# A one-hot comparison that reads f32 numbers from PSUM, in a graph network kernel on one Trainium2 core

## The reference: what is computed

```python
h = relu(layernorm(x)); x = x + L0(h)   # two SAGE layers: mean of the messages h[src] per dst
h = relu(layernorm(x)); x = x + L1(h)   # two attention layers (8 heads)
h = relu(layernorm(x)); x = x + L2(h)   # a graph transformer layer
h = relu(layernorm(x)); x = x + L3(h)   # two GIN layers: max of the messages h[src] per dst
# SAGE: agg = segment_sum(h[src], dst) / max(deg, 1);  out = relu(agg @ Wl + b + h @ Wr)
# GIN:  agg = segment_max(h[src], dst);                out = (h + agg) @ W + b
```

## Time and profile before

| what | value |
|---|---|
| median of 3 runs | 8765.62 us (8765.36, 8765.62, 8808.96) |
| span of the profiled execution | 8795.7 us; of the three runs only 8808.96 can hold it |
| busy share PE, DVE, ACT, POOL | 35%, 64%, 26%, 74% |
| chain of waits: POOL line 1644 | 48% of the span |
| passes 0 and 1 | about 90 to 1120 and 1200 to 2250 us |
| attention passes 2 to 4 | about 2360 to 6510 us |
| passes 5 and 6 | about 6630 to 7645 and 7710 to 8725 us |

### The profile page before, as it was taken

The page is one execution under the profiler, slowest core; times in us unless marked ns, Lnnn a source line. Parts: engine busy times, 40 slices in busy tenths (PEclk is TensorE's granted clock), DMA queues, the critical chain, the costliest instruction groups (busy, mean ns, idle before and its releaser), DMA issues.

```text
span 8795.7 us, 77398 instructions
## 1 busy us (share of the span) xinstructions
PE 3081.9 (35%) x15108; PEld 1692.0 (19%) x15108; DVE 5587.2 (64%) x8739; ACT 2262.0 (26%) x6542; POOL 6501.0 (74%) x5372
## 2 busy tenths in 40 slices
PE   3666656666400000200000010000025676667766
PEld 1333333333200000000000000000023343333333
DVE  5556646666477777567777757777776555455554
ACT  1000000000244444344444434444441000000000
POOL 5787768888488888568887758888856777777776
PEclk9888868888655555555555555555557887777877
DMA  2222222222244444334444434444422222222222
GB/s 81 93 93 91 94 78 90 92 90 92 90 131 130 130 132 132 105 120 130 133 130 131 126 104 125 127 127 126 126 83 79 93 94 93 88 84 94 93 91 83
DMA packets 371813, 928.59 MB, mean 106 GB/s; under 512 B 107787, under 2 KB 140629, under 8 KB 371751
## 3 DMA queue, kind: packets, MB, share of 16 engines
q0 software_dynamic: 220208, 517.27, 20.8%
q1 hardware_dynamic: 151543, 410.66, 13.0%
HBM read 520.70 MB, written 406.64 MB: 105 GB/s over the span
## 4 chain that ended last, share of the span: by engine, by line
POOL 48%; issue 26%; PE 11%; another core or an unknown queue 7%; DVE 3%; DMA 2%; SPq 1%; ACT 1%; DVEq 0%; POOLq 0%; ACTq 0%
POOL arena L1644 48%; PE bank L1384 4%; PE cin_ps L1384 2%; PE cout_ps L1384 1%; DVE outs L652 1%; PE bank L1348 1%; PE bank L1335 1%; DMA arena<-table,near_idx 1%; PE bank L1373 1%; SPq L1537 0%; PE bank L1323 0%; PE bank L1349 0%; SPq L1586 0%; PE bank L1338 0%
## 5 line engine op out<-in xcount | busy, mean ns | idle before, releaser
L1644 POOL DMA_INDIRECT arena<-table,near_idx x5002 | 5982.2, 1196 | 1857.5 <-issue 1512.4
L1384 PE MATMUL bank<-arena,work 125*128 125x384 bf16 x6750 | 1428.7, 368 | 577.7 <-DVE work L667 294.7
L1361 PE MATMUL cin_ps<-ident,tails 128*128 128x128 f32 x9 | 2.7, 438 | 3988.8 <-DVE tails L905 3988.8
L652 DVE SCALAR_TENSOR_TENSOR outs<-outs,same,arena 128x128 f32<-128x128 f32 x1568 | 547.7, 349 | 682.3 <-DMA arena<-table,near_idx 518.6
L1136 ACT ACTIVATE arena<-bank,tile_base 125x128 bf16<-125x128 f32 x432 | 158.7, 367 | 3172.3 <-remote 1461.6
L1384 PEld LDWEIGHTS bank<-arena,work 125*128 125x128 bf16 x6750 | 709.4, 107 | 1218.9 <-issue 890.7
L741 DVE TENSOR_TENSOR work<-work,arena 128x896 f32<-128x896 f32 x336 | 370.1, 1102 | 716.1 <-DMA arena<-table,near_idx 713.5
L652 DVE SCALAR_TENSOR_TENSOR outs<-outs,fence,arena 128x128 f32<-128x128 f32 x1568 | 550.0, 351 | 420.8 <-DMA arena<-table,near_idx 212.0
L781 DVE TENSOR_TENSOR_SCAN work<-work 128x1024 f32<-128x1024 f32 x336 | 770.0, 2292 | 38.9
L1361 PEld LDWEIGHTS cin_ps<-ident,tails 128*128 128x128 f32 x9 | 1.5, 213 | 3989.9 <-DVE tails L905 3989.9
L667 DVE TENSOR_TENSOR work<-arena 125x3200 bf16<-125x3200 bf16 x378 | 689.0, 1823 | 51.1 <-issue 39.9
(11 more groups left out here) (237 smaller groups left out, 4890.7 us busy)
## 6 DMA issues: line engine op xcount, KB each, us to landing
rows_plain<-outs SPq DMA_DIRECT2D x448, 448.0 KB
rows_att<-outs SPq DMA_DIRECT2D x336, 504.0 KB
arena<-table,near_idx POOLq DMA_INDIRECT x5002
table<-arena SPq DMA_DIRECT2D x18, 500.0 KB
qtable<-arena SPq DMA_DIRECT2D x33, 250.0 KB
table<-H SPq DMA_DIRECT2D x24, 250.0 KB
arena<-qtable,near_idx POOLq DMA_INDIRECT x168
arena<-rows_plain,last_i POOLq DMA_INDIRECT x100, 3.3
```

Source lines behind the costliest of these rows:

```text
L652: v.scalar_tensor_tensor(out_plain[:, s, j, :], prev, flags[:, bass.ds(first + j, 1)], row, *ops).then_inc(s_agg, 1)
L1384: ins = pe.matmul(pick_bank[u], hot_src[k][u][:, t, :], parts3[:, :, t, :], start=(t == 0), stop=(t == NB - 1))
L1644: pool.indirect_dma_start(dst, None, tab, bass.IndirectOffsetOnAxis(ap=idx, axis=0))\
```

## The change

The one-hot comparison reads the turned source numbers in PSUM itself, as f32. Each partition's 25 own node numbers are laid once a pass in `node_no` (f32, 25 elements, read with a broadcast over the 128 edges), in place of the bf16 table `tile_no` of 25 x 128. ScalarE's Relu, the tile `pick_tile`, and the semaphore `s_tile` go. Since the comparison now holds the PSUM region, a turn may write a region only when the one-hot two groups back is done, which TensorE waits for; the regions alternate between two PSUM banks.

```diff
-        tile_no = arena[0:NP, TILE_AT:TILE_AT + NB * P // 2].bitcast(BF16).rearrange("p (i e) -> p i e", e=P)
-        PICK_AT = TILE_AT + NB * P // 2
+        node_no = arena[0:NP, TILE_AT:TILE_AT + NB]
+        PICK_AT = TILE_AT + NB
...
-        source_bank = [bank[0][0:NP, u * P:(u + 1) * P] for u in range(RING)] + [hist_ps[0:NP, 0:P]]
+        source_bank = {k: [(bank[0], cout_ps if k < 2 else flag_ps)[u % 2][0:NP, 384:512] for u in range(RING)]
+                       + [hist_ps[0:NP, 0:P]] for k in PICKS}
...
             def one_hot(k, it, s):
                 for i, (u, _) in enumerate(units(k, s)):
-                    v.wait_ge(s_tile, pick_number(k, it, s) + (i + 1))
-
-                    v.tensor_tensor(hot_src[k][u], pick_tile[u].unsqueeze(1).to_broadcast([NP, NB, P]), tile_no,
+                    v.wait_ge(s_across, pick_number(k, it, s) + (i + 1))
+
+                    v.tensor_tensor(hot_src[k][u], source_bank[k][u].unsqueeze(1).to_broadcast([NP, NB, P]),
+                                    node_no.unsqueeze(2).to_broadcast([NP, NB, P]),
                                     ALU.is_equal).then_inc(s_onehot, 1)
...
-                step(v.tensor_copy(tile_no, lo_iota[0:NP, 1:NB + 1].unsqueeze(2).to_broadcast([NP, NB, P])))
+                step(v.tensor_scalar(node_no, lo_iota[0:NP, 1:NB + 1], tile_base[0:NP, 0:1], None, ALU.subtract))
...
             def number_tiles(k, it, s):
-                n = pick_number(k, it, s)
                 for u, j in units(k, s):
                     at = it * (RING * GROUP) + (s * GROUP + j)
                     act.copy(pick_src[u], src_i[:, bass.ds(at, 1)].to_broadcast([P, NP])).then_inc(s_col, 1)
-                for i, (u, _) in enumerate(units(k, s)):
-                    act.wait_ge(s_across, n + (i + 1))
-                    act.activation(pick_tile[u], source_bank[u], ACT.Relu, bias=tile_base[0:NP, 0:1])\
-                        .then_inc(s_tile, 1)
...
                 for i, (u, _) in enumerate(units(k, s)):
                     pe.wait_ge(s_col, pick_number(k, it, s) + (i + 1))
+                    if not (isinstance(it, int) and it == 1 and s < 2):
+                        seen = pick_number(k, it, s - 1) if s else pick_number(k, it - 1, RING - 1)
+                        pe.wait_ge(s_onehot, seen)
                     pe.nop(nofuse=True)
-                    pe.matmul(source_bank[u], pick_src[u], ident[:, :], start=True, stop=True)\
+                    pe.matmul(source_bank[k][u], pick_src[u], ident[:, :], start=True, stop=True)\
                         .then_inc(s_across, 1)
```

## The result

The changed kernel took 8985.8 us in the median (8984.6 to 9002.8) against 8765.5 of the kernel before (8760.9 to 8809.0), a ratio of 1.024 with an interval of 1.022 to 1.026: 2.4% slower, where 5% faster had been forecast. The profiled execution's span is 9001.2 us.

What follows compares the result with a forecast made beforehand. POOL's indirect row fetches, held back by two-SBUF-input VectorE instructions, were taken as the bound. Gains of 150 (pass 1), 130 (pass 0), 157 (passes 5 and 6), 15 and 4 sum to 456 us: 8765.6 to 8310, range 8180 to 8600.

Steps and rivals of the forecast that it cites:

- What bounds the kernel, and the fetches: POOL's row fetches bound passes 0, 1, 5, 6; VectorE instructions with two SBUF inputs hold them back, 613 us excess.
- The rival of held fetches: One remaining SBUF input still holds each fetch beside a one-hot, for 3.49 us: 812 us more, 9578 us; chance 0.11.
- The comparison: VectorE's one-hot goes from 1.82 to 3.49 us, 486 times: 812 us more VectorE work; PSUM costs nothing extra.
- Passes 0 and 1, and 5 and 6: POOL stays the bound in pass 1, VectorE becomes it in 5 and 6; gains 130, 150 and 157 us.
- What it gives POOL: Fetches beside the one-hot take 0.94 us, as beside the reduction, once it has only one SBUF input.
- 1.4 us an iteration for what is left: Passes 5 and 6: VectorE's remaining waits for TensorE's picks, making iterations 33.0 us and the gain 157 us.
- ScalarE: Relu and its wait for TensorE's turn go, unblocking near_idx; 15 us booked for the help to the picks.
- TensorE's new wait: Each turn waits for the one-hots two groups back: cost 0, bounds 0 to 0.5 us a pick, 243 us at most.
- Floors reached: TensorE never holds VectorE up in the four passes: 572 us gained, 8194 us; chance 0.12.
- Passes 5 and 6 lose: Waits for picks stay: 140 us lost there against 280 won in passes 0 and 1, 8626 us; chance 0.12.
- Same: The fetches' stretch has another cause that neither grows nor goes: time within 0.5% of 8766 us; chance 0.03.

Runs made afterwards that it cites:

- e4: Kernel before with half the change: ScalarE still writes the tile number to SBUF, as 4-byte float, and the comparison reads two 4-byte SBUF inputs; 9493 us, ratio 1.092.
- e11: The changed kernel, unedited, on chip 2: 8238 us, ratio 0.950 to the kernel before.
- e13: The changed kernel, unedited, on chip 0: 8976 us, ratio 1.022 to the kernel before.
- e18: Changed kernel on chip 0, POOL waiting for the landing after 8 and 16 fetches of an iteration and its last: 8824 us, ratio 1.003 to the kernel before.
- e10: The kernel before, unedited, run for its trace on chip 6: 8689 us, ratio 1.001.
- e15: Changed kernel on chip 0 with VectorE's loop over the plain passes' iterations written out as straight code: 8873 us, ratio 1.013 to the kernel before.
- e5: Changed kernel on chip 6 with VectorE's loop alone written out as straight code in the plain passes: 8121 us, ratio 0.935 to the kernel before.

## Why the prediction was wrong

**What bounds the kernel, and the fetches: right.** The fetch beside a comparison is 0.94 to 0.95 us in the changed kernel and 4.14 in e4, whose comparison is as long. The rival of held fetches (9578) was worked out with 812 us; e4, which holds them by another comparison as long, measured 808.

**The comparison: right.** 3485 ns for 3.49.

**Passes 0 and 1, and 5 and 6: near on the chips without stretches, wrong with them.** Forecast were iterations of 31.5, 32, 33 and 33 us. e11 has 30.8, 31.7, 31.6 and 31.7, and with 8238 to 8256 the changed kernel lies 54 to 72 us below the 8310. But the kernel before is 90 to 99 us faster there too: the gain is 411 us on chip 6 and 437 on chip 2, for 456 forecast. In the first measurement the iterations were 39.5, 39.1, 38.2 and 38.2.

**The step that failed** is "What it gives POOL". It booked the fetches' going free as nothing but gain: POOL's pitch falls from some 1.56 to 1.25 us, everything else keeps its duration. Where the stretches occur, some ten fetches at that pitch slow TensorE and VectorE to one instruction per 0.70 us until POOL pauses (e13 against e18). The held fetch had acted as such a pause, which is argued from pass 1 of the kernel before and not tested: its pitch was 1.56 and it had no stretch. After, the loop regulates itself to nearly the same rate (1.60 to 1.62 us a fetch) by slow VectorE steps, late near_idx and a waiting POOL, and pays on top. The forecast put this at nothing; it turned a gain of 411 to 437 us into a loss of 207 (chip 0, 8769 to 8976) and of 220 in the first measurement. That is a rival that I didn't have: not a wait that replaces a wait, but a freed engine that slows others by a way that no semaphore of the program shows.

**The sign had been in the trace of before.** The term "1.4 us an iteration for what is left" stood for VectorE's waits for picks in passes 5 and 6, read from the earlier trace rows as TensorE being late. TensorE was late for a large part because it stood in slow stretches, 206 and 231 us in these passes; some 60% of VectorE's waiting for picks there lies beside one. In e10, the same kernel on chip 6, the reduction's group shows no idle time at all:

```profile
L674 DVE TENSOR_REDUCE arena<-bank 128x128 f32<-128x384 f32 x324 | 178.7, 551 | 0.0
```

So in 5 and 6 the 35.8 and 36.7 us were no measure of POOL, whose own pace was 33.3. The gain there was sized at 2.8 to 3.0 us an iteration and is 1.7 on a chip without stretches (33.3 to 31.6); passes 0 and 1 gave 6.4 and 5.0 on the same chip 6 (37.1 to 30.7, 37.6 to 32.6; chip 2 has 31.7 in pass 1) where 5.3 and 5.7 were expected. That the sum comes out near is partly luck, as a gain sized too high in 5 and 6 stands against one sized too low in 0. The iterations of pass 5 before went from 24.7 to 50.1 us while pass 1 held 37.5, and I took that for TensorE's jitter.

**ScalarE: right in direction.** Its wait for TensorE is gone. Its near_idx waits now for VectorE alone. The 15 us that were booked for it were not measured apart.

**TensorE's new wait: cost nothing.** On chip 2 the pick's reduction has no idle time with it.

**The rivals.** Floors reached (8194): passes 5 and 6 did reach VectorE's chain of 31.6, which that rival was about. Passes 5 and 6 lose (8626): no. Same: no, as the comparison's contention was real. None of them gives 8986. The prediction held that by the Trainium skill's inference could not show 2.47 us. That goes further than the section, "Who interferes with whom", does: it also says that two SBUF inputs contend with a GpSimd instruction that reads SBUF, and the fetch reads near_idx there.

**What stays open.** Why the runs on chips 0 and 9 have the stretches and those on 1, 2 and 6 don't, and by which way a fetch on POOL slows an instruction on TensorE. Whether it is the chip at all is not shown: after the first measurement all runs without stretches (chips 1, 6 and 2) came first and all with them (0, 9 and 0 again) came last, and no chip was seen both ways. A state of the machine that came and went would look the same. Packets of the fetches take as long with and without stretches (245 ns in the changed kernel's pass 1, first measurement, and in e11), and they land no later in the course of a run. Nor is ten fetches a sharp bound: of the 45 stretches of the kernel before, 26 begin in runs of ten or fewer, where held fetches had already broken the count. That the first measurement came from such a chip is inferred, from 8765 against 8769 for the kernel before and from the stretches in both its traces.

## What to carry to other kernels

When a change speeds up an engine that others held back, ask what its new pace does to those that share nothing with it in the program; gaps with "issue" on two engines at once, and a spacing that is always a multiple of one number, are no part of your schedule. Run the unedited kernel beside the edited ones before you believe an experiment: here the chip had changed, and every edit seemed to cure what was not there. And a change that gains 5% on one chip and costs 2% on another has both as its result; pacing the freed engine (e18) buys the worse chip back to even (1.003). On the better one it was not measured; its iterations of 36 to 38 us against 31 to 33 there lead one to expect that most of the gain would go.

## What the hardware showed

- Two levels for the same program: the kernel before 8667 to 8692 on chips 1, 2 and 6 and 8769 to 8807 on chips 0 and 9; the changed kernel 8238 to 8256 on chips 2 and 6 and 8976 on chip 0. Chip and time of the run are not separated.
- Slow stretches: one instruction per 0.70 us on TensorE, in loops and in straight code, and on VectorE where it runs its loop with register instructions (not in e15's straight code). POOL's fetches keep their 1.25 us in them, and ScalarE's register instructions their 0.03 to 0.08. In the changed kernel they begin after about 10 fetches 1.25 us apart and end 3 us after the last; with a pause after every 8 they are gone (e18).
- A VectorE comparison with both inputs in SBUF holds back a fetch on POOL until 0.8 us after its end, at 4 bytes (4.14 us) as at 2 (2.47 in the earlier trace rows); with one input in PSUM it doesn't (0.94). The Trainium skill, "SBUF — State Buffer", section Who interferes with whom, says that one SBUF input outside the 2-port modes doesn't contend, and the changed kernel agrees. It says that two contend with a GpSimd instruction that reads SBUF, as the fetch reads near_idx, and e4 agrees; so its inference that a tensor_tensor leaves the making of descriptors alone can't be carried over to an indirect fetch.
- VectorE's register instructions are not free: with VectorE's loop written out (e5, chip 6), which takes out them and the loop's branch, passes 5 and 6 go from 31.6 to 29.3 us an iteration and the whole from 8256 to 8121.
